# Rotary attention in float16 parts: the mix of a fused two-layer Perceiver block on one Trainium2 core

## The chip, the cores and the metric

One core of one Trainium2 chip. The metric is the device time of one execution of the whole program in microseconds; smaller is better. All times below are microseconds unless marked ns.

## What is computed

The program runs two layers on x (16 sequences of 64 rows, width 256) with a context of 128 rows per sequence: in each layer a cross attention, a self attention and an FFN, each on a layer norm of x and added to x. The change touches only the self attention of the second layer, which is this part of the reference (16 heads of 128):

```python
Q = jnp.einsum('btc,ncd->btnd', x, W_Q) + b_Q
K = jnp.einsum('btc,ncd->btnd', x, W_K) + b_K
V = jnp.einsum('btc,ncd->btnd', x, W_V) + b_V
Q = _apply_rope(Q, cos, sin)
K = _apply_rope(K, cos, sin)
scores = jnp.einsum('bqnd,bknd->bnqk', Q, K) / math.sqrt(d_head)
scores = jnp.where(causal[None, None], scores, -jnp.inf)
probs = jax.nn.softmax(scores, axis=-1)
z = jnp.einsum('bnqk,bknd->bqnd', probs, V)
out = jnp.einsum('bqnd,ndm->bqm', z, W_O) + b_O
```

The "mix" is the product of probs and V.

## The kernel before

The 1024 rows of x are 8 tiles of 128 rows, two sequences to a tile. `self_attention_rotary` works in 32 units: a unit is one head of one half of x (4 tiles, 8 sequences). The first 16 units are the heads of the first half, the next 16 those of the second. Every engine runs a program of its own over steps n = 0, 1, 2, ..., each a software pipeline: step n projects unit n, scores unit n-1, mixes unit n-2 and multiplies unit n-3 by the output weights. Loops over four steps are rolled, those at the ends and in the middle are written out. Engines meet only through semaphores, and each takes its instructions strictly in the order of its program.

What each engine does in step n, in its order, with lines of the kernel before:

- PE (TensorE): k = 0 projection of unit n (line 58, the helper `accumulate`, six float16 products of 512 columns: high times high, high times low, low times high, over two chunks), scores of n-1 (line 2056, waits for both rope additions), the k = 1 projection, two transposes of the probabilities of n-2 (line 2065, float32, wait for `normed`), the output product of n-3 (line 2036, twelve float16 products), the v projection of n (line 58, 24 products of 128 columns), the mix of n-2 (line 2087, four float32 products).
- DVE (VectorE): the rope of q (line 2171, one product with the cosines, two with the sines), mask and negative maximum of the scores of n-1 (lines 2187, 2191), the rope of k, the reciprocal of the sums (line 2210), `ra_z_lo`, the low float16 part of the mixed values with the v bias (line 2214).
- ACT (ScalarE): `ra_w_hi`, the high part of the weights of unit n+2 (line 1731), two copies of the transposed probabilities out of the bank into `probs_t` (line 2123), four exponentials (line 2129), the copy of v out of the bank (line 2136), `ra_z_hi`, the high part of the mixed values with the v bias (line 2142). In steps 28 to 30 it also casts the weights of the FFN that follows.
- POOL (GpSimd): the rope's addition for q and for k (line 1995), the probabilities times the reciprocal (line 1999, signals `normed`), `ra_w_lo`, the low part of the weights of unit n+2 (line 1738, signals `w_split`). In steps 16 and 28 also the output bias onto x (line 1985).
- SP (SyncE) issues the loads, in one queue. Its iteration n waits until the low weights of unit n-2 are made (which POOL does in its step n-4), then issues the raw weights of unit n into the buffer that this frees (line 1968), the q and k bias of unit n-2 (line 1956) and the v bias of unit n-5 (line 1962), which ACT's `ra_z_hi` of step n-3 reads:

```python
if 4 <= n < UNITS:
    sp.wait_ge(loaded[n % 2], 16 * (n // 2))
    sp.wait_ge(w_split, n - 1)
    sp.dma_start(raw[n % 2][:], a["l1_attn_w"][n % H]).then_inc(loaded[n % 2], 16)
if 2 <= n - 2 < UNITS:
    load_bias(n - 2)
if 2 <= n - 5 < UNITS:
    load_v_bias(n - 5)
```

The bias load waits besides for `crossing` (DVE's sine products of unit n-4), the v bias load for `mix_kept` (the `ra_z_lo` two units earlier, whose buffer it takes).

Of the kernel before, what the change touches and what calls it, by code (L numbers as in the profile page):

```python
# [22 lines left out]
P = 128  # L23
# [23 lines left out]
def wait(eng, sem, value):  # L47

    if isinstance(value, int) and value <= 0:
        return  # L50
    eng.wait_ge(sem, value)


def accumulate(nc, out, factors):

    last = len(factors) - 1
    for n, (lhs, rhs) in enumerate(factors):
        mm = nc.tensor.matmul(out, lhs, rhs, start=(n == 0), stop=(n == last))  # L58
    return mm
# [1812 lines left out]
def self_attention_rotary(nc, g, ln):  # L1872
# [3 lines left out]

    m, a = g.m, g.a
    SCALE = 1.0 / float(np.sqrt(P))  # L1880
    HD = P // 2
    TP = TH // 2
    with ExitStack() as own:
        def sb(name, shape, dt=F32):
            return own.enter_context(nc.sbuf_tensor(f"ra_{name}", shape, dt))
# [4 lines left out]

        direct = [[sb(f"direct{f}{k}", [P, TH, P]) for k in range(2)] for f in range(2)]
        crossed = [sb(f"crossed{k}", [P, TH, P]) for k in range(2)]
        v_sb = [sb(f"v{f}", [P, TH, P]) for f in range(4)]
        masked = [sb(f"masked{f}", [P, TH, S]) for f in range(2)]
        probs = [sb(f"probs{f}", [P, TH, S]) for f in range(2)]
        probs_t = sb("probs_t", [P, TH, 2, S])
        z_hi = [sb(f"z_hi{f}", [P, TH, P], F16) for f in range(2)]
        z_lo = [sb(f"z_lo{f}", [P, TH, P], F16) for f in range(2)]
        wo_hi, wo_lo = m.ra_wo_hi, m.ra_wo_lo
# [9 lines left out]
        exped = g.sem("ra_exped")  # L1909
        inverted, normed = g.sem("ra_inverted"), g.sem("ra_normed")  # L1910
        turned, turn_kept, cleared = g.sem("ra_turned"), g.sem("ra_turn_kept"), g.sem("ra_cleared")
        mixed, z_high, mix_kept = g.sem("ra_mixed"), g.sem("ra_z_high"), g.sem("ra_mix_kept")
        summed, added = g.sem("ra_summed"), g.sem("ra_added")

        qk_bank = [g.bank[0], g.bank[1]]
        v_bank = g.bank[2][:].rearrange("p (t n) -> p t n", t=TH)
        score_bank = g.bank[3][:, 0:TH * S].rearrange("p (t n) -> p t n", t=TH)
        turn_bank = g.bank[4][:, 0:TH * S]
        mix_bank = g.bank[5][:]
        out_bank = [g.bank[k][:].rearrange("p (t n) -> p t n", t=2) for k in (6, 7)]  # L1920
        ffn = gated_ffn_steps(nc, g, own)
# [55 lines left out]
        @block.gpsimd  # L1977
        def _(pool):
            nc.gpsimd.memset(probs_t[:], 0.0).then_inc(cleared, 1)

            ln.rstd(pool, 1)

            def add_bias(half):
                rows = slice(half * TH, (half + 1) * TH)
                nc.gpsimd.tensor_tensor(out=m.x[:, rows, :], in0=m.x[:, rows, :],
                                        in1=out_bias[:].unsqueeze(1).broadcast_to([P, TH, D]),
                                        op=ALU.add).then_inc(biased, 1)

            def step(n, f, i, half):
                project, score, mix, out = stages(n)  # L1990
                e = f % 2
                if project:
                    for k in range(2):
                        pool.wait_ge(crossing, 2 * n + k + 1)
                        nc.gpsimd.tensor_tensor(out=direct[e][k][:], in0=direct[e][k][:],  # L1995
                                                in1=crossed[k][:], op=ALU.add).then_inc(roped, 1)
                if score:
                    pool.wait_ge(inverted, n)
                    nc.gpsimd.tensor_tensor(out=probs[1 - e][:], in0=probs[1 - e][:],
                                            in1=inverse[1 - e][:].unsqueeze(2).broadcast_to([P, TH, S]),  # L2000
                                            op=ALU.mult).then_inc(normed, 1)
                if not isinstance(n, int) or n + 2 < UNITS:
                    split_rotary_low(nc, g, pool, n + 2, (f + 2) % 4)
                if isinstance(n, int) and n in (H, UNITS - 4):
                    pool.wait_ge(tables, 64)
                    add_bias(0 if n == H else 1)
                if isinstance(n, int) and n == H + 3:
                    ffn.ln.rstd(pool, 0)
            unit_loop(pool, step)
            ffn.ln.rstd(pool, 1)  # L2010

        @block.tensor
        def _(pe):
# [27 lines left out]
            def step(n, f, i, half):  # L2041
                project, score, mix, out = stages(n)
                e = f % 2
                rows = slice(half * TH, (half + 1) * TH)
                if isinstance(n, int) and n == H:
                    pe.wait_ge(ln.ready, ln.ready_count)
                if project:
                    pe.wait_ge(w_split, n + 1)
                    project_to(n, f, rows, 0)
                if score:  # L2050
                    pe.wait_ge(roped, 2 * n)
                    wait(pe, limited, n - 1)
                    for t in range(TH):
                        for b in range(2):
                            at, k = slice(b * S, (b + 1) * S), t % 2
                            mm = nc.tensor.matmul(score_bank[k * HD:(k + 1) * HD, t - k + b, :], direct[1 - e][0][:, t, at],  # L2056
                                                  direct[1 - e][1][:, t, at], start=True, stop=True)
                    mm.then_inc(scored, 1)
                if project:
                    project_to(n, f, rows, 1)  # L2060
                if mix:
                    pe.wait_ge(normed, n - 1)
                    wait(pe, turn_kept, n - 2)
                    for q in range(TP):
                        mm = nc.tensor.transpose(turn_bank[:, q * P:(q + 1) * P],  # L2065
                                                 probs[e][:, 2 * q:2 * q + 2, :].rearrange("p t n -> p (t n)"),
                                                 m.ident[:])
                    mm.then_inc(turned, 1)
                if out:
                    output(n, e, half)  # L2070
                if project:
                    wait(pe, v_kept, n)
                    for t in range(TH):
                        factors = []
                        for c in range(CC):
                            xs = [x[:, c, half * TH + t, :] for x in (m.xt_hi, m.xt_lo)]
                            factors += split_factors(*xs, w_hi[f][:, 2, c, :], w_lo[f][:, 2, c, :])
                        mm = accumulate(nc, v_bank[:, t, :], factors)
                    mm.then_inc(v_done, 1)
                if isinstance(n, int) and n == 1:  # L2080
                    for k in (2, 3):
                        ln.transpose(pe, k)
                if mix:
                    pe.wait_ge(turn_kept, n - 1)
                    wait(pe, mix_kept, n - 2)
                    for t in range(TH):
                        mm = nc.tensor.matmul(mix_bank[:, t * P:(t + 1) * P], v_sb[(f + 2) % 4][:, t, :],  # L2087
                                              probs_t[:, t, :, :].rearrange("p b s -> p (b s)"),
                                              start=True, stop=True)
                    mm.then_inc(mixed, 1)  # L2090

            def begin_ffn():
# [16 lines left out]
        def _(act):  # L2109
            def step(n, f, i, half):  # L2110
# [5 lines left out]
                if mix:  # L2116
                    act.wait_ge(turned, n - 1)
                    wait(act, mixed, n - 2)
                    if isinstance(n, int) and n == 2:
                        act.wait_ge(cleared, 1)  # L2120
                    for b in range(2):
                        at = slice(b * HD, (b + 1) * HD)
                        ins = nc.scalar.activation(probs_t[at, :, b, :], turn_bank[at].rearrange("p (a s) -> p a s", a=TH), ACT.Copy)  # L2123
                    ins.then_inc(turn_kept, 1)
                if score:
                    act.wait_ge(maxed, n)
# [6 lines left out]
                if project:  # L2133
                    act.wait_ge(v_done, n + 1)
                    wait(act, mixed, n - 3)
                    nc.scalar.activation(v_sb[f][:], v_bank, ACT.Copy).then_inc(v_kept, 1)
                if mix:

                    act.wait_ge(mixed, n - 1)
# [20 lines left out]
        def _(dve):  # L2160
# [17 lines left out]
            def step(n, f, i, half):  # L2178
# [28 lines left out]
                if score:  # L2207
                    dve.wait_ge(exped, n)
                    wait(dve, normed, n - 2)
                    nc.vector.reciprocal(inverse[1 - e][:], total[1 - e][:]).then_inc(inverted, 1)  # L2210
                if mix:

                    dve.wait_ge(z_high, n - 1)
                    nc.vector.scalar_tensor_tensor(z_lo[e][:].rearrange("p t n -> p (t n)"), mix_bank,  # L2214
                                                   v_bias[e][:], z_hi[e][:].rearrange("p t n -> p (t n)"),
                                                   ALU.add, ALU.subtract).then_inc(mix_kept, 1)
# [209 lines left out]
```

## Time and profile before

| what | us |
| --- | --- |
| median of 3 runs (809.97 to 816.26) | 816.07 |
| the profiled execution, its own time | 814.12 |
| its span, first to last instruction | 812.3 |
| PE busy in the span | 699.4 |
| DVE busy | 586.6 |
| ACT busy | 426.0 |
| POOL busy | 369.1 |
| rotary attention, from its first instructions to the last `ra_z_lo` | 523.2 to 769.5 |

The profile is of one execution. Busy time is the sum of an engine's records; PE's records overlap each other, since matmuls are pipelined and their ends are modelled, so that a stretch can read as fully busy with a small wait in it. The start-to-start distance of PE's instructions is the better measure of what they take. A wait is put down to the engine or the DMA whose semaphore came last.

### The profile page before, as it was taken

The page shows a single profiled execution, that of the slowest core. Times are in us where ns is not written, and L with a number is a line of the kernel's source. Part 1 is how long each engine was busy: PE and PEld are TensorE (multiplying, and loading weights), DVE is VectorE, ACT ScalarE, POOL GpSimd, SP SyncE. Part 2 cuts the span into 40 slices and gives each one's busy share as a digit, 9 for nine tenths or more (in the row PEclk, how much of TensorE's full clock was granted, in tenths as well). Part 3 has the DMA queues.
Part 4 walks back from the last instruction along what each step waited for, and adds up shares of the span by engine and source line. Part 5 has one row for each costly group of instructions (what it writes and reads, how often), then busy time and mean ns, then how long its engine had stood idle before and what let it go on. Part 6 is the DMA issues. An engine that isn't in the chain of part 4 may idle for free. (4 is left out here: it accounts for less than half of the span.)

```text
span 812.3 us, 16000 instructions
## 1 busy us (share of the span) xinstructions
PE 699.4 (86%) x5487; PEld 467.8 (58%) x5490; DVE 586.6 (72%) x1152; ACT 426.0 (52%) x1314; POOL 369.1 (45%) x313
## 2 busy tenths in 40 slices
PE   4997899789558679999995898879999999999786
PEld 3665576479424444444433676547777777777544
DVE  3356687676778756666674888598888898888577
ACT  1465788434258622122244877145555664558764
POOL 3500545246135314443485544256666676666200
PEclk9999899999769769999997999899999999999989
DMA  9445000000030030622010000012211233131001
GB/s 240 128 145 185 1 3 1 1 1 2 1 91 1 1 110 1 193 75 70 1 40 0 2 1 2 1 40 61 60 48 50 59 112 112 40 109 22 1 1 53
DMA packets 33572, 41.92 MB, mean 52 GB/s; under 512 B 15072, under 2 KB 23264, under 8 KB 32608
## 3 DMA queue, kind: packets, MB, share of 16 engines
q1 hardware_dynamic: 33504, 41.06, 17.2%
q8 instruction: 37, 0.61, 0.3%
q14 instruction: 31, 0.25, 0.1%
HBM read 40.00 MB, written 1.05 MB: 51 GB/s over the span
## 5 line engine op out<-in xcount | busy, mean ns | idle before, releaser
L1995 POOL TENSOR_TENSOR ra_direct<-ra_direct,ra_crossed 128x512 f32<-128x512 f32 x64 | 81.2, 1269 | 79.4 <-DVE ra_crossed L2171 79.3
L695 POOL TENSOR_TENSOR c_probs<-c_probs,c_inverse 128x512 f32<-128x512 f32 x64 | 65.6, 1039 | 74.3 <-DVE c_inverse L711 74.3
L2171 DVE SCALAR_TENSOR_TENSOR ra_crossed<-bank,ra_bias,ra_sin 64x512 f32<-64x512 f32 x128 | 95.9, 750 | 1.9
L670 ACT ACTIVATE c_probs<-bank,c_neg_max 128x128 f32<-128x128 f32 x256 | 89.9, 390 | 5.3 <-DVE c_neg_max L729 5.3
L1460 POOL TENSOR_TENSOR r_turned<-r_times_a,r_times_b 128x1024 f32<-128x1024 f32 x24 | 56.4, 2349 | 72.0 <-DVE r_times_b L1659 72.0
L670 ACT ACTIVATION_READ_ACCUMULATOR c_probs<-bank,c_neg_max 128x1 f32 x256 | 59.2, 231 | 0.0
L2123 ACT ACTIVATE ra_probs_t<-bank 64x256 f32<-64x256 f32 x64 | 24.1, 377 | 61.4 <-PE bank L2065 61.1
L1738 POOL TENSOR_TENSOR ra_w_lo<-ra_raw,ra_w_hi 128x768 f16<-128x768 f32 x32 | 52.7, 1645 | 0.0
L2129 ACT ACTIVATE ra_probs<-ra_masked,ra_neg_max 128x64 f32<-128x64 f32 x128 | 43.0, 337 | 17.5 <-DVE ra_neg_max L2191 17.3
L58 PE MATMUL bank<-xt_hi,ra_w_hi 128*128 128x512 f16 x128 | 49.3, 385 | 1.6 <-DVE ra_crossed L2171 0.9
L621 PE MATMUL bank<-c_probs_t,c_keys 128*64 128x512 f32 x128 | 37.3, 663 | 14.0 <-DVE c_probs_t L721 11.8
L721 DVE COPY c_probs_t<-bank 128x512 f32<-128x512 f32 x64 | 43.2, 677 | 8.1 <-PE bank L603 8.0
L58 PE MATMUL bank<-xt_hi,ra_w_lo 128*128 128x512 f16 x128 | 49.0, 383 | 0.0
L58 PE MATMUL bank<-xt_lo,ra_w_hi 128*128 128x512 f16 x128 | 49.0, 383 | 0.0
L2171 DVE SCALAR_TENSOR_TENSOR ra_direct<-bank,ra_bias,ra_cos 128x512 f32<-128x512 f32 x64 | 47.6, 744 | 0.3 <-PE bank L58 0.2
L2214 DVE SCALAR_TENSOR_TENSOR ra_z_lo<-bank,ra_v_bias,ra_z_hi 128x512 f16<-128x512 f32 x32 | 24.0, 749 | 29.3 <-ACT ra_z_hi L2142 29.3
L58 PE MATMUL bank<-ra_w_hi,xt_hi 128*128 128x128 f16 x256 | 44.7, 220 | 0.0
L58 PE MATMUL bank<-ra_w_lo,xt_hi 128*128 128x128 f16 x256 | 44.7, 219 | 0.0
L58 PE MATMUL bank<-ra_w_hi,xt_lo 128*128 128x128 f16 x256 | 44.6, 219 | 0.0
L729 DVE TENSOR_REDUCE c_neg_max<-bank 128x4 f32<-128x512 f32 x64 | 40.8, 678 | 2.5 <-PE bank L58 2.5
L58 PE MATMUL bank<-kvt_hi,l_q_stack 128*128 128x128 f16 x256 | 35.0, 231 | 7.5 <-PEq L1416 4.5
L603 PE MATMUL bank<-ident_sb,c_probs 128*128 128x128 f32 x256 | 37.1, 289 | 5.0 <-POOL c_probs L695 5.0
(271 smaller groups left out, 2087.2 us busy)
## 6 DMA issues: line engine op xcount, KB each, us to landing
ra_raw<-l_attn_w_dram SPq DMA_DIRECT2D x32, 384.0 KB, 3.1
wq<-l_wq_dram SPq DMA_DIRECT2D x16, 256.0 KB, 2.9
wo<-l_wo_dram SPq DMA_DIRECT2D x16, 256.0 KB, 3.2
wkcq<-l_wkcq_dram SPq DMA_DIRECT2D x16, 192.0 KB, 2.9
ra_wo<-l_attn_wo_dram SPq DMA_DIRECT2D x1, 2048.0 KB, 10.1
wqr<-l_wqr_dram SPq DMA_DIRECT2D x16, 96.0 KB, 3.0
x_res<-x_dram SPq DMA_DIRECT2D x2, 512.0 KB, 4.7
wkv<-l_wkv_dram SPq DMA_DIRECT2D x16, 64.0 KB, 2.8
```

Source lines behind the costliest of these rows:

```text
L58: mm = nc.tensor.matmul(out, lhs, rhs, start=(n == 0), stop=(n == last))
L603: mm = nc.tensor.transpose(turn_bank[q][:, n, :], probs[u][:, q * HP + n, :], m.ident[:])
L621: mm = nc.tensor.matmul(mix_view[e * DC:(e + 1) * DC], keys[u][:], probs_t[u][:, :, e * S:(e + 1) * S], start=True, stop=True)
L670: e = nc.scalar.activation(probs[u][:, n, :], score_bank[u][q][:, n - q * HP, :], ACT.Exp, bias=neg_max[u][:, n:n + 1], accum_out=total[u] ...
L695: nc.gpsimd.tensor_tensor(out=probs[u][:, at, :], in0=probs[u][:, at, :], in1=inverse[u][:, at].unsqueeze(2).broadcast_to([P, HP, L]), op= ...
L721: nc.vector.tensor_copy(probs_t[u][:, at, :], turn_bank[q]).then_inc(turn_kept, 1)
L729: nc.vector.tensor_reduce(neg_max[u][:, at], score_bank[u][q], AX.X, ALU.max, negate=True).then_inc(maxed, 1)
L1460: nc.gpsimd.tensor_tensor(out=turned[k % 3][:], in0=times_a[k % 2][:], in1=times_b[k % 2][:], op=ALU.add).then_inc(rotated, 1)
L1738: nc.gpsimd.tensor_tensor(out=m.ra_w_lo[f][:], in0=m.ra_raw[f % 2][:], in1=m.ra_w_hi[f][:], op=ALU.subtract).then_inc(g.ra_split, 1)
L1995: nc.gpsimd.tensor_tensor(out=direct[e][k][:], in0=direct[e][k][:], in1=crossed[k][:], op=ALU.add).then_inc(roped, 1)
L2129: ins = nc.scalar.activation(probs[1 - e][:, t, :], masked[1 - e][:, t, :], ACT.Exp, bias=neg_max[1 - e][:, t:t + 1], scale=-1.0, accum_ou ...
L2171: ins = nc.vector.scalar_tensor_tensor(dst[out_lo:out_lo + rows].rearrange("p t (b s) -> p (t b) s", b=2), src[lo:lo + rows], bias[e][lo:l ...
```

## The change

The mix becomes three float16 products instead of one float32 product, as the projections already are. For that both factors are split into a high part (rounded to float16) and a low part (the rest, in float16):

- POOL makes the high part of the normalised probabilities, then the normalised probabilities in float32, then the difference as the low part, each waiting for the one before; the last one signals `normed`.
- PE transposes both parts (four float16 transposes instead of two float32 ones, with a float16 identity that POOL copies once at the start) into one bank read as float16.
- ACT copies both out into `probs_t`, which has twice the elements at half the size; the copy of v writes float16 (`v_hi`).
- DVE subtracts `v_hi` from the bank to give `v_lo`, between the reciprocal and `ra_z_lo`, and signals `v_kept` in ACT's place.
- PE mixes with twelve products (high high, high low, low high for each of four tiles).

```diff
@@ POOL
+            nc.gpsimd.tensor_copy(ident[:], m.ident[:]).then_inc(cleared, 1)
...
                 if score:
                     pool.wait_ge(inverted, n)
+                    wait(pool, turned, n - 2)
+                    nc.gpsimd.tensor_tensor(out=probs_hl[1 - e][:, 0], in0=probs[1 - e][:],
+                                            in1=inverse[1 - e][:].unsqueeze(2).broadcast_to([P, TH, S]),
+                                            op=ALU.mult).then_inc(rounded, 1)
+                    pool.wait_ge(rounded, n)
                     nc.gpsimd.tensor_tensor(out=probs[1 - e][:], in0=probs[1 - e][:],
                                             in1=inverse[1 - e][:].unsqueeze(2).broadcast_to([P, TH, S]),
-                                            op=ALU.mult).then_inc(normed, 1)
+                                            op=ALU.mult).then_inc(scaled, 1)
+                    pool.wait_ge(scaled, n)
+                    nc.gpsimd.tensor_tensor(out=probs_hl[1 - e][:, 1], in0=probs[1 - e][:],
+                                            in1=probs_hl[1 - e][:, 0], op=ALU.subtract).then_inc(normed, 1)
@@ PE
-                    for q in range(TP):
-                        mm = nc.tensor.transpose(turn_bank[:, q * P:(q + 1) * P],
-                                                 probs[e][:, 2 * q:2 * q + 2, :].rearrange("p t n -> p (t n)"),
-                                                 m.ident[:])
+                    for part in range(2):
+                        for q in range(TP):
+                            at = (part * TP + q) * P
+                            mm = nc.tensor.transpose(turn_bank[:, at:at + P],
+                                                     probs_hl[e][:, part, 2 * q:2 * q + 2, :]
+                                                     .rearrange("p t n -> p (t n)"), ident[:])
...
-                        mm = nc.tensor.matmul(mix_bank[:, t * P:(t + 1) * P], v_sb[(f + 2) % 4][:, t, :],
-                                              probs_t[:, t, :, :].rearrange("p b s -> p (b s)"),
-                                              start=True, stop=True)
+                        hi, lo = (v[(f + 2) % 4][:, t, :] for v in (v_hi, v_lo))
+                        p_hi, p_lo = (probs_t[:, part, t, :, :].rearrange("p b s -> p (b s)") for part in range(2))
+                        mm = accumulate(nc, mix_bank[:, t * P:(t + 1) * P], split_factors(hi, lo, p_hi, p_lo))
@@ ACT
-                        ins = nc.scalar.activation(probs_t[at, :, b, :], turn_bank[at].rearrange("p (a s) -> p a s", a=TH), ACT.Copy)
+                        ins = nc.scalar.activation(probs_t[at, :, :, b, :].rearrange("p h a s -> p (h a) s"),
+                                                   turn_bank[at].rearrange("p (a s) -> p a s", a=2 * TH), ACT.Copy)
...
-                    nc.scalar.activation(v_sb[f][:], v_bank, ACT.Copy).then_inc(v_kept, 1)
+                    nc.scalar.activation(v_hi[f][:], v_bank, ACT.Copy).then_inc(v_high, 1)
@@ DVE
+                if project:
+                    dve.wait_ge(v_high, n + 1)
+                    nc.vector.tensor_tensor(v_lo[f][:], v_bank, v_hi[f][:], ALU.subtract).then_inc(v_kept, 1)
```

POOL's order in one step of the rolled loop, before (two rope additions, the scaling, the low weights):

```order
L1994 ISA
L1995 TENSOR_TENSOR ra_direct<-ra_direct,ra_crossed 128x512
L1994 REGISTER_ALU
L1995 TENSOR_TENSOR ra_direct<-ra_direct,ra_crossed 128x512
L1999 TENSOR_TENSOR ra_probs<-ra_probs,ra_inverse 128x256
L1737 REGISTER_ALU
L1738 TENSOR_TENSOR ra_w_lo<-ra_raw,ra_w_hi 128x768
```

and the same step after, where `ra_probs_hl` holds both parts:

```order
L2000 ISA
L2001 TENSOR_TENSOR ra_direct<-ra_direct,ra_crossed 128x512
L2000 REGISTER_ALU
L2001 TENSOR_TENSOR ra_direct<-ra_direct,ra_crossed 128x512
L2006 TENSOR_TENSOR ra_probs_hl<-ra_probs,ra_inverse 128x256
L2010 TENSOR_TENSOR ra_probs<-ra_probs,ra_inverse 128x256
L2014 TENSOR_TENSOR ra_probs_hl<-ra_probs,ra_probs_hl 128x256
L1737 REGISTER_ALU
L1738 TENSOR_TENSOR ra_w_lo<-ra_raw,ra_w_hi 128x768
```

Two operations have come in between the second rope addition and the low weights; nothing else moved on POOL, and SP's order is the same in both.

DVE's order from the maximum of one step to `ra_z_lo`, before (the step in which the statistics of the next layer norm are made):

```order
L2191 TENSOR_REDUCE ra_neg_max<-ra_masked 128x4
L2171 SCALAR_TENSOR_TENSOR ra_direct<-bank,ra_bias,ra_cos 128x512
L2171 SCALAR_TENSOR_TENSOR ra_crossed<-bank,ra_bias,ra_sin 64x512 x2
L83 BN_STATS all_stats<-x_res 128x6 x4
L86 BN_AGGR all_moments<-all_stats 128x2 x4
L89 TENSOR_SCALAR all_var<-all_moments 128x4
L2210 RECIPROCAL ra_inverse<-ra_total 128x4
L2214 SCALAR_TENSOR_TENSOR ra_z_lo<-bank,ra_v_bias,ra_z_hi 128x512
```

and after:

```order
L2210 TENSOR_REDUCE ra_neg_max<-ra_masked 128x4
L2190 SCALAR_TENSOR_TENSOR ra_direct<-bank,ra_bias,ra_cos 128x512
L2190 SCALAR_TENSOR_TENSOR ra_crossed<-bank,ra_bias,ra_sin 64x512 x2
L83 BN_STATS all_stats<-x_res 128x6 x4
L86 BN_AGGR all_moments<-all_stats 128x2 x4
L89 TENSOR_SCALAR all_var<-all_moments 128x4
L2229 RECIPROCAL ra_inverse<-ra_total 128x4
L2232 TENSOR_TENSOR ra_v_lo<-bank,ra_v_hi 128x512
L2236 SCALAR_TENSOR_TENSOR ra_z_lo<-bank,ra_v_bias,ra_z_hi 128x512
```

One subtraction has come in behind the reciprocal and in front of `ra_z_lo`; in the other steps it stands at the same place, without the statistics.

## Rows read from the trace of the kernel before

**Rows 1.** Windows: start:end, length, busy of each engine, granted clock, DMA share, GB/s.

```profile
core 0: us, PE busy (x) PEld busy (x) DVE busy (x) ACT busy (x) POOL busy (x), PEclk, DMA share, GB/s
561.40:654.40 93.00, 93.00 (x963) 69.92 (x961) 79.35 (x130) 54.65 (x169) 63.22 (x54) 1.00 0.22 58
727.00:768.00 41.00, 36.23 (x368) 27.71 (x367) 29.85 (x51) 33.07 (x75) 22.01 (x19) 1.00 0.06 12
```

**Rows 2.** Waits between 545 and 760 us: us in total, times, longest.

```profile
POOL ra_direct L1995 <- DVE ra_crossed L2171: 71.9, 55, 2.9
...
ACT ra_z_hi L2142 <- DMA ra_v_bias<-l_attn_bv_dram: 3.2, 4, 1.1
```

**Rows 3.** Instructions in order of time, two steps: start, us, engine, line, idle before.

```profile
561.38 0.69 ACT L2142 ACTIVATE ra_z_hi<-bank,ra_v_bias 128x512 f16<-128x512 f32 x1 [0.42 <-DMA ra_v_bias<-l_attn_bv_dram]
...
562.10 0.75 DVE L2214 SCALAR_TENSOR_TENSOR ra_z_lo<-bank,ra_v_bias,ra_z_hi 128x512 f16<-128x512 f32 x1 [1.14 <-ACT ra_z_hi L2142]
...
565.92 0.22 PE L58 MATMUL bank<-ra_w_hi,xt_hi 128*128 128x128 f16 x1
...
567.26 1.11 PE L2087 MATMUL bank<-ra_probs_t,ra_v 128*128 128x128 f32 x8
...
568.17 0.18 DVE L2210 RECIPROCAL ra_inverse<-ra_total 128x4 f32<-128x4 f32 x1
568.20 0.38 PE L58 MATMUL bank<-xt_hi,ra_w_hi 128*128 128x512 f16 x1
...
568.21 1.27 POOL L1995 TENSOR_TENSOR ra_direct<-ra_direct,ra_crossed 128x512 f32<-128x512 f32 x1 [1.83 <-DVE ra_crossed L2171]
...
569.44 0.61 POOL L1999 TENSOR_TENSOR ra_probs<-ra_probs,ra_inverse 128x256 f32<-128x256 f32 x1
...
570.01 1.64 POOL L1738 TENSOR_TENSOR ra_w_lo<-ra_raw,ra_w_hi 128x768 f16<-128x768 f32 x1
...
571.56 0.38 PE L2065 MATMUL bank<-ident_sb,ra_probs 128*128 128x128 f32 x2
...
572.62 0.38 SPq L1962 DMA_DIRECT2D ra_v_bias<-l_attn_bv_dram  x1
...
575.66 0.69 ACT L2142 ACTIVATE ra_z_hi<-bank,ra_v_bias 128x512 f16<-128x512 f32 x1 [0.44 <-PE bank L2087]
```

**Rows 4.** The tile ra_v_bias: its loads in this stage, and landing times.

```profile
L1962 SPq DMA_DIRECT2D ra_v_bias<-l_attn_bv_dram x30: 328/382/392, 558.3 to 761.6; - x30
...
DMA to landing us min/median/max: 2.0/2.6/4.6
```

**Rows 5.** ACT in order of time: ra_z_hi of units 0, 26 and 29.

```profile
547.01 0.68 ACT L2142 ACTIVATE ra_z_hi<-bank,ra_v_bias 128x512 f16<-128x512 f32 x1
...
735.88 0.69 ACT L2142 ACTIVATE ra_z_hi<-bank,ra_v_bias 128x512 f16<-128x512 f32 x1 [1.07 <-DMA ra_v_bias<-l_attn_bv_dram]
...
760.10 0.68 ACT L2142 ACTIVATE ra_z_hi<-bank,ra_v_bias 128x512 f16<-128x512 f32 x1
```

**Rows 6.** Groups by line: busy us, mean ns of one, idle before.

```profile
L1999 POOL TENSOR_TENSOR ra_probs<-ra_probs,ra_inverse 128x256 f32<-128x256 f32 x32 | 19.6, 613 | 5.6 <-DVE ra_inverse L2210 5.5
L1738 POOL TENSOR_TENSOR ra_w_lo<-ra_raw,ra_w_hi 128x768 f16<-128x768 f32 x32 | 52.7, 1645 | 0.0
L123 DVE TENSOR_TENSOR xt_lo<-bank,xt_hi 128x512 f16<-128x512 f32 x16 | 10.7, 687 | 10.7 <-ACT xt_hi L119 10.6
L2123 ACT ACTIVATE ra_probs_t<-bank 64x256 f32<-64x256 f32 x64 | 24.1, 377 | 61.4 <-PE bank L2065 61.1
```

**Rows 7.** POOL in order of time: two dependent operations in the first layer.

```profile
21.29 2.34 POOL L182 TENSOR_TENSOR kv<-kv,kv_crossed 128x1024 f32<-128x1024 f32 x1
23.72 2.78 POOL L186 TENSOR_SCALAR kv<-kv 128x1024 f32<-128x1024 f32 x1
```

**Rows 8.** The last units, in order of time, and the copy of v.

```profile
567.46 0.60 ACT L2136 ACTIVATE ra_v<-bank 128x512 f32<-128x512 f32 x1
...
765.25 0.77 ACT L2123 ACTIVATE ra_probs_t<-bank 64x256 f32<-64x256 f32 x2 [0.53 <-PE bank L2065]
...
766.89 1.06 PE L2087 MATMUL bank<-ra_probs_t,ra_v 128*128 128x128 f32 x8
```

More of the change, by code:

```diff
@@ L1892, in self_attention_rotary @@
         crossed = [sb(f"crossed{k}", [P, TH, P]) for k in range(2)]
-        v_sb = [sb(f"v{f}", [P, TH, P]) for f in range(4)]
+        v_hi = [sb(f"v_hi{f}", [P, TH, P], F16) for f in range(4)]
+        v_lo = [sb(f"v_lo{f}", [P, TH, P], F16) for f in range(4)]
         masked = [sb(f"masked{f}", [P, TH, S]) for f in range(2)]
         probs = [sb(f"probs{f}", [P, TH, S]) for f in range(2)]
-        probs_t = sb("probs_t", [P, TH, 2, S])
+        probs_hl = [sb(f"probs_hl{f}", [P, 2, TH, S], F16) for f in range(2)]
+        probs_t = sb("probs_t", [P, 2, TH, 2, S], F16)
+        ident = sb("ident", [P, P], F16)
         z_hi = [sb(f"z_hi{f}", [P, TH, P], F16) for f in range(2)]
@@ L1911, in self_attention_rotary @@
         turned, turn_kept, cleared = g.sem("ra_turned"), g.sem("ra_turn_kept"), g.sem("ra_cleared")
+        scaled, rounded, v_high = g.sem("ra_scaled"), g.sem("ra_rounded"), g.sem("ra_v_high")
         mixed, z_high, mix_kept = g.sem("ra_mixed"), g.sem("ra_z_high"), g.sem("ra_mix_kept")
@@ L1917, in self_attention_rotary @@
         score_bank = g.bank[3][:, 0:TH * S].rearrange("p (t n) -> p t n", t=TH)
-        turn_bank = g.bank[4][:, 0:TH * S]
+        turn_bank = g.bank[4][:].bitcast(F16)[:, 0:2 * TH * S]
         mix_bank = g.bank[5][:]
@@ L2063, in step @@
                     wait(pe, turn_kept, n - 2)
-                    for q in range(TP):
-                        mm = nc.tensor.transpose(turn_bank[:, q * P:(q + 1) * P],
-                                                 probs[e][:, 2 * q:2 * q + 2, :].rearrange("p t n -> p (t n)"),
-                                                 m.ident[:])
+                    if isinstance(n, int) and n == 2:
+                        pe.wait_ge(cleared, 2)
+                    for part in range(2):
[4 more added lines that the diff above has]
+                                                     .rearrange("p t n -> p (t n)"), ident[:])
                     mm.then_inc(turned, 1)
```

## The prediction

> **What bounds the kernel now.** I read four views, in this order. The table of windows first: between 561.4 and 654.4 us, which is steady rotary attention, the records cover the whole of PE and 79.35 of 93.00 us of DVE, and TensorE's granted clock is 1.00, the 2.4 GHz level [rows 1]. So PE alone looks like the bound. Its records overlap, so I went to the instructions in order of time for one pair of steps [rows 3], and there the stage is a ring. ra_z_hi starts at 561.38 and again at 575.66, two steps later: 14.28 us, 7.14 a step. Between them everything on DVE runs back to back: ra_z_lo from 562.10, two ropes, mask and maximum, until the reciprocal ends at 568.35. POOL starts its second rope addition at 568.21, scales the probabilities at 569.44, makes the low part of the weights from 570.01 to about 571.65, and only then SP may issue its three loads; the last of them, the v bias (0.5 KB), goes out at 572.62. That bias is an operand of ra_z_hi of the step after.
>
> Third, the tile ra_v_bias: its load lands 2.0 to 4.6 us after issue, median 2.6 [rows 4]. From 572.62 that is 575.22 plus 0.05 of handover, and ra_z_hi starts at 575.66. So the ring SP -> DMA -> ACT -> DVE -> POOL -> SP has about 0.4 us of slack in 14.28, and four times in the stage it has none: the list of waits shows ra_z_hi waiting for that DMA, 3.2 us in all [rows 2]. POOL itself looks idle there: 71.9 us of waiting for DVE's crossed product. That idle time stands before the first half of POOL's step, not behind its second half, so it can't cover what is added behind the second addition.
>
> **The change, part by part.** All of it is per unit, 32 units.
>
> PE, mix: four float32 products take 567.26 to 568.20, 0.94 us; twelve float16 ones at the pace of the v projection ((567.26 - 565.92) / 24 = 0.056) take 0.67. Gain 0.27 [rows 3]. Transposes: four float16 ones of 128 columns at 0.056 are 0.22, in place of two float32 ones; taken as no change. Not a gain of the stage while the ring above is longer than PE's work.
>
> DVE, v_lo: a subtraction bank minus f16 of 128x512 is xt_lo's form, 0.69 us [rows 6]. It stands between the reciprocal (end 568.35) and ra_z_lo. DVE's step would be 568.35 - 562.10 = 6.25, plus 0.69, plus 0.02: 6.96, still under 7.14. Its cover is the idle time before ra_z_lo. Cost 0. It waits for v_high on ACT, which ends before the reciprocal in most steps; behind it only ra_z_lo is queued. If that cover were gone the step could not fall below 6.96.
>
> ACT: v_hi is the same size as the copy it replaces, 0.60 [rows 8]. Each of the two copies into ra_probs_t goes from 64x256 to 64x512; that 128x512 copy out of a bank is 0.60, the 64x256 one 0.38, so at most 0.22 more each, 0.44 a unit, and at least nothing; I take the 0.44, since the copy's time goes with its columns in these two rows [rows 6]. In the steady stretch ACT has idle time in front of its exponentials, so I cost it only where ACT is the bound.
>
> POOL: one multiplication (0.61) becomes three dependent operations. The first two have the old shape, 0.61 each. The third reads two full streams and is not in the trace. From below it is 0.55 by ra_w_lo's rate (1645 ns x 256/768), which also subtracts float16 from float32 [rows 6]; from above 0.64, half of the 1.27 of the rope addition [rows 3]; I take 0.61, the row of the same shape. Each waits for the one before through a semaphore: such a pair on POOL shows 23.72 - 21.29 - 2.34 = 0.09 between end and start [rows 7], I take 0.08, where two independent ones overlap by 0.04. Now 569.44 to 570.01 is 0.57; then 3 x 0.61 + 2 x 0.08 - 0.04 = 1.95. Added: 1.38 us; with the ends of the third operation, and a wait of 0 to 0.15, 1.2 to 1.6.
>
> What is queued behind it: ra_w_lo (1.64), whose semaphore SP waits for before the raw weights; behind those in SP's queue stand the qk bias and the v bias. All shift by 1.38. The transposes wait too: they start at 571.56 on PE, and the split ends at 569.44 + 1.99 = 571.43, just in time.
>
> The ring with it: 572.62 - 561.38 = 11.24, plus 1.38, plus a landing of 2.6, plus 0.05 = 15.27 us for two steps, against 14.28: the 0.4 of slack is used up and 1.0 is left over, 0.5 a unit. A step is then 7.64 us, and PE, which now needs 0.27 less than its 7.14, idles about 0.8 of it. That doesn't cost clock: between 727 and 768 us PE is busy 36.23 of 41.00 with gaps of that size, and the granted clock stays at 1.00 [rows 1].
>
> The load's landing is the least certain term. [...] The trace has 2.0 as its smallest landing and 2.6 as its median [rows 4]. [...]
>
> **The sum.** From the first ra_z_hi (547.01) to that of unit 26 (735.88) [rows 5] are 13 rings, 188.9 us; 13 x 14.28 = 185.6, so 3.2 us are irregular steps (bias addition on POOL, statistics on DVE, late loads). After: 13 x 15.27 = 198.5, +9.6 if the longer ring swallows the irregular steps, +12.8 if it keeps them. The additions on busy DVE and POOL stay, so I take +11.5. Units 26 to 29 (735.88 to 760.10, 24.2 us for three) are bound by ACT, which also casts the FFN weights: 3 x 0.44 = +1.3. Head: the exponentials of the first step with a mix wait behind the longer copies, +0.5. Tail: in the last two steps nothing hides POOL and ACT: 2 x (1.38 + 0.44) - 0.27 for the mix, less the 0.87 by which the copy (end 766.02) now precedes the mix (766.89) [rows 8], less 0.3 of small slack: +2.2. Together +15.5. The profiled execution took 814.12 us (span 812.3), which gives 829.6; the median of the three runs is 816.07, and these range from 809.97 to 816.26, so I say 830.5.
>
> **Rivals.** A, forecast: the v bias ring, 830.5. Its own range: landings of 2.0 to 3.3 give -7.8 to +9.1 for 13 rings, with POOL's 1.2 to 1.6 about 2.5 either way; not all at once, so 820 to 840.
>
> B, not slower: the load isn't what releases ra_z_hi, because landing or SP's order has more room than I read. For it: 28 of 32 units show no such wait. Against: 0.4 us of slack is an easy figure, and the four waits. PE then gains 0.27 and the step closes at DVE's 6.96: -0.18 x 29 = -5.2, with +4.0 for head, ACT and tail, and 0.9 as above between execution and median: 814. It takes over from the point where POOL adds less than the 0.4 us of slack, or the landing is under 1.6.
>
> C, little change: the bias has room as in B, but ra_v_lo, which waits for v_hi on ACT and stands in front of ra_z_lo, comes late by the 0.2 that would be gained, so that the step keeps its 7.14. For it: ACT's longer copies push its exponentials and with them v_hi. Against: 0.44 of them fall into ACT's idle time. Only the +4.0 is left: 819.
>
> D, slower than A: the float16 forms on POOL, or a landing of 3.3 as at the four waits, make the ring 16 us; the transposes then wait as well. 13 x (16 - 14.28) = 22.4, with +4.0 and the 0.9: 841, and above where the irregular steps are kept.
>
> **How the numbers follow.** A 0.76, B 0.07, C 0.09, D 0.08. The measurement tells about 1% from no change. Of A a little (0.04) lies under 824, the +1% line; so slower is 0.82, same 0.15, faster 0.03, the last from B with a short landing. The range 819 to 841 holds A, C's value and about half of D.
>
> **What would show it.** Right: ra_z_hi's waits put down to the DMA ra_v_bias in most units, 0.5 to 1 us each; steps of 7.6 us; POOL's three operations at 1.9 to 2.0 us; about 0.8 us of idle PE before the scores, released by POOL; granted clock 1.00 throughout. Wrong: ra_z_hi still released by the mix, or ra_v_lo holding ra_z_lo back, or steps near 7.0.

## The result, and the profile after

| | before | after |
| --- | --- | --- |
| median, us | 816.16 (809.97 to 820.49, 4 runs) | 829.09 (826.26 to 832.95, 4 runs) |
| ratio, 95% interval | | 1.0196 [1.0149, 1.0242] |
| span of the profiled execution | 812.3 | 827.4 |

The kernel became slower. The two medians are 12.9 us apart (1.6%), the ratio puts it at 1.5 to 2.4%, which is 12 to 20 us; 14.4 were forecast, which lies inside that.

The same views as before, of the kernel after. First the windows of the steady part, which answer to [rows 1]:

```profile
core 0: us, PE busy (x) PEld busy (x) DVE busy (x) ACT busy (x) POOL busy (x), PEclk, DMA share, GB/s
561.40:654.40 93.00, 84.71 (x964) 60.71 (x963) 81.69 (x134) 56.33 (x157) 71.92 (x74) 1.00 0.19 51
```

PE is busy 84.71 of 93.00 us where it was busy throughout, at the same granted clock, and no engine is full. A stage in which no engine is full has a loop in it, and the list of waits (545 to 775 us) says where; it answers to [rows 2]:

```profile
POOL ra_direct L2001 <- DVE ra_crossed L2190: 43.8, 33, 1.9
...
ACT ra_z_hi L2161 <- DMA ra_v_bias<-l_attn_bv_dram: 24.4, 25, 1.9
...
DVE ra_z_lo L2236 <- ACT ra_z_hi L2161: 18.7, 20, 1.8
```

The wait for the v bias was 3.2 us in four steps and is 24.4 us in 25. In order of time, two steps that answer to [rows 3] (ACT, DVE, POOL, PE and SP from the timeline of each, put together by their start):

```profile
591.17 0.69 ACT L2161 ACTIVATE ra_z_hi<-bank,ra_v_bias 128x512 f16<-128x512 f32 x1 [1.07 <-DMA ra_v_bias<-l_attn_bv_dram]
...
591.89 0.75 DVE L2236 SCALAR_TENSOR_TENSOR ra_z_lo<-bank,ra_v_bias,ra_z_hi 128x512 f16<-128x512 f32 x1 [1.07 <-ACT ra_z_hi L2161]
...
598.01 1.26 POOL L2001 TENSOR_TENSOR ra_direct<-ra_direct,ra_crossed 128x512 f32<-128x512 f32 x1 [1.82 <-DVE ra_crossed L2190]
598.05 0.66 DVE L2232 TENSOR_TENSOR ra_v_lo<-bank,ra_v_hi 128x512 f16<-128x512 f32 x1
...
599.23 0.62 POOL L2006 TENSOR_TENSOR ra_probs_hl<-ra_probs,ra_inverse 128x256 f16<-128x256 f32 x1
599.32 0.73 PE L2070 MATMUL bank<-ra_direct 128*64 128x64 f32 x16 [1.15 <-POOL ra_direct L2001]
599.92 0.61 POOL L2010 TENSOR_TENSOR ra_probs<-ra_probs,ra_inverse 128x256 f32<-128x256 f32 x1
600.61 0.67 POOL L2014 TENSOR_TENSOR ra_probs_hl<-ra_probs,ra_probs_hl 128x256 f16<-128x256 f32 x1
601.24 1.65 POOL L1738 TENSOR_TENSOR ra_w_lo<-ra_raw,ra_w_hi 128x768 f16<-128x768 f32 x1
601.34 0.40 PE L2083 MATMUL bank<-ra_ident,ra_probs_hl 128*128 128x128 f16 x4
601.78 1.20 ACT L2141 ACTIVATE ra_probs_t<-bank 64x512 f16<-64x512 f16 x2 [1.98 <-PE bank L2083]
...
603.85 0.38 SPq L1967 DMA_DIRECT2D ra_v_bias<-l_attn_bv_dram  x1
...
606.52 0.69 ACT L2161 ACTIVATE ra_z_hi<-bank,ra_v_bias 128x512 f16<-128x512 f32 x1 [1.47 <-DMA ra_v_bias<-l_attn_bv_dram]
```

This is the ring closed. From ra_z_hi at 591.17 to the issue of the v bias at 603.85 are 12.68 us, where 11.24 stood before; the load needs 2.67 more until ra_z_hi starts, and nothing else is waited for. Two steps take 15.35 us; the pair one step later (598.38 to 613.63) takes 15.25. Of the 13 pairs from unit 0 to unit 26 the median is 15.35 too, and the longest, in the middle of the stage, is 16.71.

The landings of the tile ra_v_bias, which answer to [rows 4], are as they were, and ra_z_hi of units 0, 26, 29 and 31, which answer to [rows 5], give the length of the parts:

```profile
DMA to landing us min/median/max: 1.9/2.6/4.7
```

```profile
545.30 0.68 ACT L2161 ACTIVATE ra_z_hi<-bank,ra_v_bias 128x512 f16<-128x512 f32 x1
...
746.94 0.69 ACT L2161 ACTIVATE ra_z_hi<-bank,ra_v_bias 128x512 f16<-128x512 f32 x1 [0.94 <-DMA ra_v_bias<-l_attn_bv_dram]
...
772.46 0.68 ACT L2161 ACTIVATE ra_z_hi<-bank,ra_v_bias 128x512 f16<-128x512 f32 x1
...
784.15 0.69 ACT L2161 ACTIVATE ra_z_hi<-bank,ra_v_bias 128x512 f16<-128x512 f32 x1 [2.43 <-PE bank L58]
```

The 26 steps to unit 26 take 201.64 us (188.87 before, +12.8), the three to unit 29 take 25.52 (24.22, +1.3), the last two 11.69 (7.88, +3.8).

### The profile page after: what moved, and what is told of

It reads as the page before. It is cut to its first block and busy times, and to the rows that moved or that the text cites. A ratio compares the mean times of both kernels' runs of the same rounds, so it can differ in the third digit from the quotient of the medians.

```text
span 827.4 us, 16532 instructions
## 1 busy us (share of the span) xinstructions
PE 693.0 (84%) x5679; PEld 455.8 (55%) x5682; DVE 605.3 (73%) x1184; ACT 440.3 (53%) x1314; POOL 410.3 (50%) x378
## 5 line engine op out<-in xcount | busy, mean ns | idle before, releaser
L2141 ACT ACTIVATE ra_probs_t<-bank 64x512 f16<-64x512 f16 x64 | 37.9, 592 | 50.4 <-PE bank L2083 50.0
L2070 PE MATMUL bank<-ra_direct 128*64 128x64 f32 x512 | 23.9, 233 | 26.9 <-POOL ra_direct L2001 26.7
L2070 PEld LDWEIGHTS bank<-ra_direct 128*64 128x64 f32 x512 | 19.4, 139 | 42.0 <-POOL ra_direct L2001 34.4
```

The source lines that it names most:

```text
L2141: ins = nc.scalar.activation(probs_t[at, :, :, b, :].rearrange("p h a s -> p (h a) s"), turn_bank[at].rearrange("p (a s) -> p a s", a=2 * ...
```

## The experiments

The theory is the ring of the prediction: ra_z_hi, DVE's step, POOL's second addition, what POOL does until its low weights are made, SP's three loads, the landing, ra_z_hi. Its rivals are DVE's added subtraction, ACT's longer copies, transposes waiting for the split, and POOL's load as such. All kernels are compared with the kernel before on the same chip. What is measured in the profile, of one execution each, is the distance between ra_z_hi of unit 0 and of unit 26, and the mean step between units 5 and 15:

| kernel | 26 steps, us | mean step | ratio to before, interval |
| --- | --- | --- | --- |
| before | 188.87 | 7.17 | |
| after | 201.64 | 7.81 | 1.0196 [1.0149, 1.0242] |
| after, v bias first | 186.01 | 7.04 | 0.9986 [0.9949, 1.0022] |
| before, v bias first | 187.57 | 7.17 | 0.9997 [0.9958, 1.0036] |
| before, POOL's split alone | 202.90 | 7.69 | 1.0269 [1.0223, 1.0316] |
| before, extra work behind | 190.44 | 7.17 | 1.0004 [0.9962, 1.0045] |
| before, one extra operation | 193.99 | 7.34 | 1.0069 [1.0033, 1.0105] |
| after, low weights between | 185.44 | 7.03 | 0.9965 [0.9924, 1.0005] |
| after, both moves | 185.73 | 7.03 | 1.0030 [0.9989, 1.0072] |
| after, v bias next | 191.25 | 7.25 | 1.0114 [1.0075, 1.0154] |
| after, v bias first, no v_lo | 184.90 | 7.00 | 0.9975 [0.9937, 1.0012] |

The 7.81 of the kernel after is longer than half of 15.35, because its stretch ends with a pair of 16.24 (644.75 to 660.99), in which the issue came 0.5 later and the load took 3.0 until ra_z_hi.

**The v bias first, in the kernel after.** SP's loop has its two ends exchanged. The bias of a unit then goes out ahead of the wait for the low weights that it stood behind, right after the two loads of the iteration before, and so one step earlier:

```diff
+                if 2 <= n - 5 < UNITS:
+                    load_v_bias(n - 5)
                 if 4 <= n < UNITS:
                     sp.wait_ge(loaded[n % 2], 16 * (n // 2))
                     sp.wait_ge(w_split, n - 1)
                     sp.dma_start(raw[n % 2][:], a["l1_attn_w"][n % H]).then_inc(loaded[n % 2], 16)
                 if 2 <= n - 2 < UNITS:
                     load_bias(n - 2)
-                if 2 <= n - 5 < UNITS:
-                    load_v_bias(n - 5)
```

> The kernel after, but SP issues each v bias ahead of the raw weights, so that it no longer stands behind the wait for POOL's low weights. Theory of the v bias ring: no wait of ra_z_hi for that DMA is left, the 26 steps from the first ra_z_hi on fall from 201.6 us to 182 to 187 (DVE's 6.96 to 7.1 a step), and the time from 829 to 811 to 816. Rival, that the transposes waiting for the split probabilities, or DVE's added subtraction, hold the step: steps stay at 7.6 to 7.7 us and the time at 827 to 830.

Measured 812.35 us (809.18 to 817.73). The 26 steps lose 15.6 us, and no wait for that DMA is left. The load lands no faster (median still 2.6 us), it has room: one goes out at 600.66, while the ra_z_hi that reads it starts at 608.81.

```profile
600.66 0.38 SPq L1967 DMA_DIRECT2D ra_v_bias<-l_attn_bv_dram  x1
```

The whole loss of the change is gone with the change still in. What stands behind the ring shows in DVE's timeline, one step from ra_z_lo to ra_z_lo:

```profile
588.70 0.75 DVE L2236 SCALAR_TENSOR_TENSOR ra_z_lo<-bank,ra_v_bias,ra_z_hi 128x512 f16<-128x512 f32 x1
589.37 0.74 DVE L2190 SCALAR_TENSOR_TENSOR ra_direct<-bank,ra_bias,ra_cos 128x512 f32<-128x512 f32 x1
...
594.77 0.18 DVE L2229 RECIPROCAL ra_inverse<-ra_total 128x4 f32<-128x4 f32 x1
594.86 0.66 DVE L2232 TENSOR_TENSOR ra_v_lo<-bank,ra_v_hi 128x512 f16<-128x512 f32 x1
595.52 0.75 DVE L2236 SCALAR_TENSOR_TENSOR ra_z_lo<-bank,ra_v_bias,ra_z_hi 128x512 f16<-128x512 f32 x1
```

From its ra_z_lo to the next, 6.82 us, DVE is not kept waiting once. Such steps alternate with steps of 7.2 to 7.3, in which it waits some tenths around ra_v_lo. In the windows table it is busy 89.24 of 93.00 us, that is 6.76 of the mean step of 7.04:

```profile
561.40:654.40 93.00, 90.95 (x1046) 65.97 (x1043) 89.24 (x146) 61.69 (x169) 79.67 (x80) 1.00 0.24 64
```

**The v bias first, in the kernel before.** The same edit.

> The kernel before with the same move of the v bias load. Theory of the ring: before, the load had about 0.4 us of room in most steps, so only the four waits of 3.2 us in all go; 812 to 816. Rival, that the ring already set the pace before (steps of 7.17): they fall to PE's 7.07 or less and the time to 810 or less.

Measured 812.89 us (807.78 to 820.42), and the same step of 7.17. So the ring did not set the pace before; it had its room of a few tenths, as read from [rows 3].

**POOL's split alone, in the kernel before.** The three operations and their waits are put in; the parts go to a spare tile:

```diff
-                    nc.gpsimd.tensor_tensor(out=probs[1 - e][:], in0=probs[1 - e][:],
+                    nc.gpsimd.tensor_tensor(out=spare[:, 0], in0=probs[1 - e][:],
                                             in1=inverse[1 - e][:].unsqueeze(2).broadcast_to([P, TH, S]),
-                                            op=ALU.mult).then_inc(normed, 1)
+                                            op=ALU.mult).then_inc(rounded, 1)
+                    pool.wait_ge(rounded, n)
+                    nc.gpsimd.tensor_tensor(out=probs[1 - e][:], in0=probs[1 - e][:],
+                                            in1=inverse[1 - e][:].unsqueeze(2).broadcast_to([P, TH, S]),
+                                            op=ALU.mult).then_inc(scaled, 1)
+                    pool.wait_ge(scaled, n)
+                    nc.gpsimd.tensor_tensor(out=spare[:, 1], in0=probs[1 - e][:],
+                                            in1=spare[:, 0], op=ALU.subtract).then_inc(normed, 1)
```

> The kernel before with POOL's part of the change alone: its three dependent operations in place of the one, the float16 parts written to a spare tile that nothing reads; transposes, mix, ACT and DVE as before. Theory of the ring: all of the loss in the steps is there, 26 steps take 199 to 203 us and the time is 827 to 832. Rival, that the loss comes from ACT's longer copies or DVE's subtraction: under 820.

Measured 833.4 us (829.09 to 835.57), a little over the range; 26 steps in 202.90. PE, ACT and DVE have the same instructions as before, and the list of waits (545 to 765 us) has the same entry as the kernel after:

```profile
ACT ra_z_hi L2151 <- DMA ra_v_bias<-l_attn_bv_dram: 26.1, 23, 2.6
```

**The same work behind the low weights, in the kernel before.** Two operations of these shapes, the second waiting for the first, on spare tiles:

```diff
                     split_rotary_low(nc, g, pool, n + 2, (f + 2) % 4)
+                if score:
+                    pool.wait_ge(scaled, n + 1)
+                    nc.gpsimd.tensor_tensor(out=spare[:, 0], in0=spare_p[:],
+                                            in1=spare_s[:].unsqueeze(2).broadcast_to([P, TH, S]),
+                                            op=ALU.mult).then_inc(rounded, 1)
+                    pool.wait_ge(rounded, n)
+                    nc.gpsimd.tensor_tensor(out=spare[:, 1], in0=spare_p[:],
+                                            in1=spare[:, 0], op=ALU.subtract).then_inc(scaled, 1)
```

> The kernel before with two extra operations of the same shapes and the same dependence on POOL, on spare tiles, but behind the low weights, so that POOL does nearly the same work a step (1.4 us more than before) and SP isn't held up by it. Theory of the ring: POOL's place counts and not its load, 815 to 819. Rival, that POOL's load as such costs: 826 or more.

Measured 815.26 us (808.9 to 825.45), ratio 1.0004; ra_z_hi waits for the v bias 3.9 us in four steps, about as before. The last experiment and this one differ in the place of the work, not in its size, and are 2.6% apart. The place decides two things, when SP may issue and when the transposes may start; that the first counts is shown by the v bias moved first, where the transposes still wait for the split. POOL's wait for DVE's crossed product, 71.9 us in [rows 2], is halved here, since most of the added work (1.4 us in each of 32 steps) falls into it:

```profile
POOL ra_direct L2001 <- DVE ra_crossed L2185: 35.7, 30, 2.1
```

**One extra operation instead of two, in the kernel before.**

```diff
                     pool.wait_ge(inverted, n)
+                    nc.gpsimd.tensor_tensor(out=spare[:], in0=probs[1 - e][:],
+                                            in1=inverse[1 - e][:].unsqueeze(2).broadcast_to([P, TH, S]),
+                                            op=ALU.mult).then_inc(rounded, 1)
+                    pool.wait_ge(rounded, n)
```

> The kernel before with one extra operation on POOL instead of two, in front of the scaling and waited for (0.61 + 0.08 us), its result unused. Theory of the ring, by its sum: 11.25 + 0.69 + 2.65 = 14.6 us for two steps, 0.25 over before, so 26 steps in 191 to 194 us and 815 to 819. Rival, that the loss goes with POOL's added work in proportion (half of the 14 us that two operations cost): 26 steps in 195 to 197 us, 820 or more. Rival, that there is no ring but a threshold elsewhere: no change, 188 to 190 us.

Measured 819.0 us (813.24 to 827.08); 26 steps in 193.99, the upper end of the ring's range and 1.0 us below the rival's. The first 0.7 us on the ring cost 5.1 us in 26 steps, the second 8.9. The mean steps separate the two better: 7.34, where the ring's sum gives 7.30 and half of the way from 7.17 to 7.69 would be 7.43. So the cost is not proportional, as a ring with slack in it wants, but the margin is small.

**The low weights between the two rope additions, in the kernel after.**

```diff
                                                 in1=crossed[k][:], op=ALU.add).then_inc(roped, 1)
+                        if k == 0 and (not isinstance(n, int) or n + 2 < UNITS):
+                            split_rotary_low(nc, g, pool, n + 2, (f + 2) % 4)
...
-                if not isinstance(n, int) or n + 2 < UNITS:
-                    split_rotary_low(nc, g, pool, n + 2, (f + 2) % 4)
```

> The kernel after with POOL's low weights moved between its two rope additions, into the idle time there (1.8 us before the second addition, 1.65 us of work); SP's order as in the change. Theory of the ring: SP's three loads go out before the split probabilities are made, the bias arrives in time, DVE sets the pace as with the bias first (26 steps in 185 to 188 us), 811 to 816. Rival, that the place of the bias in SP's queue matters and not POOL's order: steps of 7.4 us or more, over 822.

Measured 812.48 us (810.37 to 816.15). No wait of ra_z_hi for the v bias is left here either: the ring is broken from POOL's end instead of SP's, with a step of 7.03.

**Both moves.** The edits of the first experiment and of the last one together.

> The kernel after with both moves: the v bias issued first, the low weights between the additions. Theory: either alone breaks the ring, and DVE at 7.0 us a step stands behind it, so both give no more than one: 810 to 816. Rival, that the additions' order holds up something else too: 808 or less.

Measured 816.17 us (811.85 to 821.2); 26 steps in 185.73, as with one move. The time is 0.2 us over the expected 816 at most, far less than the scatter of its executions, and nothing was gained by the second move; the two intervals, 0.9965 [0.9924, 1.0005] and 1.0030 [0.9989, 1.0072], don't put one above the other.

**The v bias behind the wait, but first of the three loads, in the kernel after.**

```diff
                     sp.wait_ge(w_split, n - 1)
+                if 2 <= n - 5 < UNITS:
+                    load_v_bias(n - 5)
+                if 4 <= n < UNITS:
                     sp.dma_start(raw[n % 2][:], a["l1_attn_w"][n % H]).then_inc(loaded[n % 2], 16)
                 if 2 <= n - 2 < UNITS:
                     load_bias(n - 2)
-                if 2 <= n - 5 < UNITS:
-                    load_v_bias(n - 5)
```

> The kernel after with the v bias still behind SP's wait for the low weights, but issued as the first of the three loads, ahead of the 384 KB of raw weights. Theory of the ring: its part on SP and the DMA shrinks by 0.9 us of issue, and the landing by some tenths (2.0 to 2.6), so the ring is 13.9 to 14.45 us for two steps, just under or over DVE's 14.08: 26 steps in 185 to 190 us, 811 to 817. Rival, that the wait for the low weights as such holds the step, whatever stands behind it: 200 us and 827 or more.

Measured 819.35 us (816.66 to 824.54): a miss, between the two. 26 steps in 191.25. The v bias now lands in a median of 2.0 us (561 to 740 us), and ra_z_hi doesn't wait for it. But two other loads of the same queue have moved back by one issue, and each of them is waited for:

```profile
ACT ra_w_hi L1731 <- DMA ra_raw<-l_attn_w_dram: 17.9, 22, 1.3
...
DVE ra_direct L2191 <- DMA ra_bias<-l_attn_b_dram: 5.5, 14, 0.5
```

The DVE entry lies on its busy chain:

```profile
601.08 0.75 DVE L2237 SCALAR_TENSOR_TENSOR ra_z_lo<-bank,ra_v_bias,ra_z_hi 128x512 f16<-128x512 f32 x1
602.34 0.75 DVE L2191 SCALAR_TENSOR_TENSOR ra_direct<-bank,ra_bias,ra_cos 128x512 f32<-128x512 f32 x1 [0.51 <-DMA ra_bias<-l_attn_b_dram]
```

The 26 steps are 5.2 us longer than with the bias first, and DVE's waits add up to 5.5. So the rows say that the wait for the low weights holds the step there too, only through the next loads behind it; no run takes these waits away by themselves.

**Without v_lo, v bias first.** DVE's subtraction and the product with it are left out:

```diff
-                        mm = accumulate(nc, mix_bank[:, t * P:(t + 1) * P], split_factors(hi, lo, p_hi, p_lo))
+                        mm = accumulate(nc, mix_bank[:, t * P:(t + 1) * P], [(hi, p_hi), (hi, p_lo)])
...
-                if project:
-                    dve.wait_ge(v_high, n + 1)
-                    nc.vector.tensor_tensor(v_lo[f][:], v_bank, v_hi[f][:], ALU.subtract).then_inc(v_kept, 1)
```

> The kernel after with the v bias first, without the low part of the values: DVE's subtraction is left out, and with it the third product of the mix (8 of 12 matmuls stay), so the mix uses values rounded to float16. Theory that DVE is the bound once the ring is gone: steps fall from 7.04 by up to the 0.66 of the subtraction until PE's own work (about 6.6) or the chain over scores and mix (6.8 to 6.9) stops them; 26 steps in 174 to 181 us, 802 to 808. Rival, that DVE isn't the bound: 810 or more.

Measured 813.87 us (808.75 to 821.54): a miss. DVE has 0.66 us less to do in each step and the step falls by 0.04. The profiled execution is the longest of its ten, but it lost that ahead of the stage, which begins at 529.78 here and at 520.59 in the profile with v_lo; in the steady stretch its granted clock is 1.00. DVE idles now before ra_z_lo, and the timelines of two steps show one more ring, right behind DVE's:

```profile
604.02 0.75 DVE L2233 SCALAR_TENSOR_TENSOR ra_z_lo<-bank,ra_v_bias,ra_z_hi 128x512 f16<-128x512 f32 x1 [0.35 <-ACT ra_z_hi L2161]
...
610.14 1.27 POOL L2001 TENSOR_TENSOR ra_direct<-ra_direct,ra_crossed 128x512 f32<-128x512 f32 x1 [0.48 <-DVE ra_crossed L2190]
611.37 0.62 POOL L2006 TENSOR_TENSOR ra_probs_hl<-ra_probs,ra_inverse 128x256 f16<-128x256 f32 x1
...
613.59 0.39 PE L2083 MATMUL bank<-ra_ident,ra_probs_hl 128*128 128x128 f16 x4
614.01 1.20 ACT L2141 ACTIVATE ra_probs_t<-bank 64x512 f16<-64x512 f16 x2 [1.40 <-PE bank L2083]
615.38 0.35 ACT L2148 ACTIVATE ra_probs<-ra_masked,ra_neg_max 128x64 f32<-128x64 f32 x1 [0.17 <-DVE ra_neg_max L2210]
...
617.34 0.68 ACT L2161 ACTIVATE ra_z_hi<-bank,ra_v_bias 128x512 f16<-128x512 f32 x1
618.05 0.75 DVE L2233 SCALAR_TENSOR_TENSOR ra_z_lo<-bank,ra_v_bias,ra_z_hi 128x512 f16<-128x512 f32 x1 [0.31 <-ACT ra_z_hi L2161]
```

DVE's ropes after ra_z_lo, POOL's addition, its split, the transposes, ACT's copies, the exponentials, v_hi, ra_z_hi: 14.03 us for two steps, 7.0 each. It runs through the change's own additions on POOL and ACT. Two steps with the bias first mostly took 14.0 to 14.2 as well, so this ring may already be what holds them, and DVE's own work is not shown to be. That this ring is what stops the step is read from the rows and was not tested by shortening it.

## Why the prediction was right

**The ring was the cause.** Giving its one link room (v bias first) takes the loss away, and so does taking the low weights out from behind the split; putting POOL's part alone into the kernel before brings the loss; the same work behind the low weights costs nothing. The rivals B and C fell with the first of these, since both say that the bias isn't in the way. Rival D's transposes do start only when the split ends (600.61 + 0.67 = 601.28, then 601.34), but the split ends as PE gets there, and no slower ring came of it.

**The ring's terms.** POOL's three operations took 601.24 - 599.23 = 2.01 us against the forecast 1.95: the two of the old shape 0.62 and 0.61, the subtraction 0.67 and not 0.61, just above the end of 0.64 that I had set for it, and 0.07 and 0.08 between end and start, as taken. With the 0.57 of before, 1.44 was added instead of 1.38. The median landing stayed at 2.6. Ring forecast 15.27, measured 15.35 in the median of 13 pairs.

The landing is 2.0 in the median when the bias is the first of the three loads, and 2.6 when 384 KB of raw weights go out 0.9 us ahead of it. The Trainium skill (DMA: Bandwidth & Descriptors, Anatomy of one DMA) fits a DMA on the gpsimd path at a fixed 2.0 us plus bytes over 436 GB/s, an estimate of 2.0 for this load. SP issues the loads here, so the fit is not for them; the first of the three agrees with its figure all the same, the one behind the raw weights does not.

**The sum.**

| term | forecast | measured in the profiles |
| --- | --- | --- |
| head, stage's first memset to first ra_z_hi | +0.5 | +1.15 (25.00 against 23.85) |
| 26 steps | +11.5 | +12.8 |
| three steps bound by ACT | +1.3 | +1.3 |
| last two steps | +2.2 | +3.8 |
| before the stage, and behind the last ra_z_hi | 0 | -3.9 |
| together | +15.5 | +15.1 |

The last line agrees partly by luck. The stage began 2.9 us earlier in this execution than in that of before (520.30 against 523.16), in parts of the program that the change doesn't touch, and the part behind the last ra_z_hi took 1.0 less. The stage itself lost 19.0, not 15.5. Medians are the better measure, and executions of one kernel scatter by more than these terms' errors.

The 26 steps: the choice between +9.6 and +12.8 (irregular steps swallowed or kept) should have been the upper end; they were kept (201.64 is 2.1 more than 13 median pairs, 188.87 was 2.3 more than 13 of its own, 14.35 each). ACT's two copies went from 0.77 to 1.20 us, 0.43 a unit, and gave +1.3 in three steps as worked out; with POOL's split alone, without these copies, the three steps stay at 24.22.

**The tail was mis-sized, in two terms.** I had taken PE's clock as constant, and its falls cost more than the 1.6 us missing; the work on POOL and ACT was put too high. In its last steps PE waited 2.28 us before scores and 1.28 and 2.01 us before transposes, where the kernel before has waits of 1.88, 0.78, 0.35 and 0.97, and the granted clock fell twice, to near 1.2 GHz; the windows of the kernel after:

```profile
773.50:776.90 3.40, 2.52 (x14) 1.92 (x15) 1.20 (x3) 1.84 (x6) 0.75 (x2) 0.53 0.04 5
780.40:783.70 3.30, 3.30 (x24) 2.65 (x22) 0.00 (x0) 1.19 (x2) 0.00 (x0) 0.52 0.00 0
```

The kernel before with the bias first prices it: the same instructions between the same ra_z_hi, 9.2 us long at a mean clock of 0.81 where the kernel before has 7.9 at 1.00:

```profile
758.80:768.00 9.20, 7.59 (x62) 6.32 (x63) 2.43 (x5) 4.20 (x16) 1.43 (x3) 0.81 0.02 2
```

So such a fall is worth about 1.3 us in these two steps, and it also comes without the change. The changed kernel was seen with one fall and with two: with the bias first the last two steps took 9.97, as the change came 11.69, and most of the difference (1.5) lies between the last transposes and the last ra_z_hi, in the second fall:

```profile
757.60:767.70 10.10, 7.16 (x75) 5.85 (x76) 3.03 (x6) 5.30 (x16) 3.68 (x6) 0.83 0.02 2
772.50:784.20 11.70, 8.41 (x75) 6.76 (x75) 3.03 (x6) 5.19 (x16) 3.56 (x6) 0.71 0.01 1
```

With one fall on either side, the change costs 9.97 - 9.21 = 0.8 us there and not the 2.2 of the forecast; the rest of the 3.8 is the clock. Which part of the 2.2 found cover is open. In the steady part the forecast held: 8 us in 93 of PE's time idle, and the clock at 1.00 throughout.

**The step behind the ring.** DVE's step was forecast as 6.96, as a bound. It took 6.82 where DVE wasn't kept waiting (the subtraction was 0.66 and not 0.69), and the mean was 7.04. That DVE sets this pace is not borne out: with 0.66 less to do it gave 7.00. Even without the v bias ring the change turns 7.17 into 7.04 and gives that back in the head, the ACT steps and the tail: no version of it here is measurably faster than the kernel before.

## What to carry to other kernels

An idle engine has room only at the place in its order where it idles: POOL waited 71.9 us in this stage, and 1.4 us of work cost 2.7% in one place and nothing in another. Follow a steady stage once around, from an instruction to its next one, through the load queues too, and note the slack of each loop; here three loops lay within 0.2 us of each other, so that removing one bound showed the next. A small load that stands in a queue behind a wait for a large one inherits that wait; issue it ahead of the wait, since ahead of the large load alone gave back only 10.4 of the 15.6 us in the 26 steps.

## What was not expected of the hardware

The landing of a load of 0.5 KB differed with what is in front of it in the same queue: median 2.6 us with 384 KB issued 0.9 us before, 2.0 us ahead of it. And the same instructions at the end of the stage took 7.9 us in the kernel before and 9.2 in the one that differs from it only in SP's order, with PE's granted clock at 1.00 or a mean of 0.81. In the second the clock fell right behind PE's wait of 1.88 us before the scores, and was at its lower level from 760 to 763 us; the first has the same wait of 1.88, and its clock stayed at 1.00. What decides between the two is not shown.
